# First matmul of four expert passes as half precision pairs, their matrices split during attention

## The reference, cut to what matters

```python
# attention: queries from layernorm(x), keys and values from layernorm(x) and from the context
sim  = einsum('bihd,bjhd->bhij', q1, concat([k1, k2])) * 64 ** -0.5
out  = einsum('bhij,bjhd->bihd', softmax(sim), concat([v1, v2]))
x    = x + tanh(g_xattn[0]) * (out.reshape(B, N1, h * d) @ Wo + bo)
# experts, on xf = layernorm(x): two of eight by the gate, and the shared one
for e in range(8):
    h   = gelu(xf @ w1[e] + b1[e])            # exact gelu
    out = out + combine[:, e:e + 1] * (h @ w2[e] + b2[e])
shared = gelu(xf @ ws1 + bs1) @ ws2 + bs2
x      = x + tanh(g_ffn[0]) * (out + shared)
```

## Time and profile before

| | |
|---|---|
| median of 3 runs | 157.3 us (156.89 to 157.64) |
| the profiled execution | 156.95 us, span of its trace 155.1 us |
| PE busy | 143.9 us (93%) |
| ACT busy | 115.1 us (74%) |
| POOL busy | 107.9 us (70%) |
| DVE busy | 103.5 us (67%) |
| granted TensorE clock | 1.00 over the span |

### The profile page before, as it was taken

One profiled execution on the slowest core, in us unless ns is written; L12 is line 12 of the kernel. 1 busy time (PEld: TensorE's weight loads), 2 busy tenths in 40 slices (PEclk: granted clock), 3 DMA queues, 4 the chain that ended last, 5 costly groups with the idle time before them and its releaser, 6 DMA issues.

```text
span 155.1 us, 4389 instructions
## 1 busy us (share of the span) xinstructions
PE 143.9 (93%) x1804; PEld 111.4 (72%) x1804; DVE 103.5 (67%) x215; ACT 115.1 (74%) x191; POOL 107.9 (70%) x95
## 2 busy tenths in 40 slices
PE   7789699979899999999898799999999999999992
PEld 5434354547566667657686698999999999989992
DVE  0779898888777686887763363834643779896631
ACT  3466789998988988887859988645567598968720
POOL 5506999777676667857798878965398089688730
PEclk9999999999999999999999999999999999999999
DMA  5679996000000000000000000030000000100001
GB/s 139 200 268 276 277 351 208 1 4 0 4 2 8 0 4 0 4 0 4 0 4 0 4 0 4 16 119 0 4 0 0 6 2 9 29 0 0 4 0 34
DMA packets 10253, 7.71 MB, mean 50 GB/s; under 512 B 1101, under 2 KB 8442, under 8 KB 10234
## 3 DMA queue, kind: packets, MB, share of 16 engines
q1 hardware_dynamic: 10234, 7.44, 15.8%
HBM read 7.18 MB, written 0.26 MB: 48 GB/s over the span
## 4 chain that ended last, share of the span: by engine, by line
PE 73%; DVE 10%; ACT 9%; issue 2%; DMA 2%; POOL 1%; SPq 0%; DVEq 0%; ACTq 0%
PE banks L1279 12%; PE banks L991 10%; PE banks L993 9%; PE banks L992 9%; PE banks L1242 5%; DVE part L821 4%; PE banks L1170 4%; ACT prob L646 3%; PE banks L1172 3%; PE banks L1171 3%; PE banks L1120 3%; PE banks L1190 2%; ACT v_hi L635 2%; DMA wf<-in_ctx_dram 2%; ACT p_hi L654 2%
## 5 line engine op out<-in xcount | busy, mean ns | idle before, releaser
L554 POOL TENSOR_TENSOR p_lo<-prob,p_hi 128x1024 f16<-128x1024 f32 x23 | 49.0, 2133 | 15.7 <-ACT p_hi L654 15.5
L710 ACT ACTIVATE prob<-banks,b1T 128x256 f32<-128x256 f32 x72 | 28.4, 475 | 12.8 <-PE banks L993 9.3
L646 ACT ACTIVATE prob<-banks 128x1024 f32<-128x1024 f32 x24 | 24.6, 1023 | 8.1 <-PE banks L1138 8.1
L821 DVE TENSOR_REDUCE part<-banks 128x2 f32<-128x1024 f32 (+1 forms) x24 | 29.0, 1216 | 1.1 <-PE banks L1093 1.0
L654 ACT ACTIVATE p_hi<-prob 128x1024 f16<-128x1024 f32 x24 | 25.4, 1057 | 0.8
L569 POOL TENSOR_TENSOR k_both<-prob,k_both 128x1024 f16<-128x1024 f32 x8 | 17.6, 2194 | 4.2 <-ACT k_both L718 3.2
L1279 PE MATMUL banks<-ring,prob 128*128 128x128 f32 x160 | 19.6, 276 | 0.0
L1170 PEld LDWEIGHTS banks<-v_hi,p_hi 128*128 128x128 f16 x192 | 17.4, 98 | 2.9 <-issue 2.5
L1170 PE MATMUL banks<-v_hi,p_hi 128*128 128x65 f16 x192 | 19.2, 195 | 0.0
L1171 PE MATMUL banks<-v_lo,p_hi 128*128 128x64 f16 x192 | 19.1, 193 | 0.0
L1172 PE MATMUL banks<-v_hi,p_lo 128*128 128x65 f16 x192 | 19.1, 194 | 0.0
(11 more groups left out here) (155 smaller groups left out, 343.8 us busy)
## 6 DMA issues: line engine op xcount, KB each, us to landing
ring<-in_L_ffn_w_dram SPq DMA_DIRECT2D x16, 256.0 KB, 5.3
wf<-in_ctx_dram SPq DMA_DIRECT2D x2, 256.0 KB, 5.3
ring<-in_L_xattn_Wk_dram SPq DMA_DIRECT2D x2, 256.0 KB, 4.7
ring<-in_L_xattn_Wv_dram SPq DMA_DIRECT2D x2, 256.0 KB, 7.1
ring<-in_L_ffn_ws_dram SPq DMA_DIRECT2D x2, 256.0 KB, 6.7
x_sb<-in_x_dram SPq DMA_DIRECT2D x1, 256.0 KB, 3.0
ring<-in_L_xattn_Wq_dram SPq DMA_DIRECT2D x1, 256.0 KB, 5.0
wo<-in_L_xattn_Wo_dram SPq DMA_DIRECT2D x1, 256.0 KB, 7.8
```

Source lines behind the costliest of these rows:

```text
L554: nc.gpsimd.tensor_tensor(p_lo[:, u % RINGP, :, :].rearrange("p a n -> p (a n)"), prob[:, u % RINGE, :], p_hi[:, u % RINGP, :, :].rearrang ...
L646: nc.scalar.activation(prob[:, u % RINGE, :], units(u).rearrange("p a n -> p (a n)"), ACT.Exp, scale=DH ** -0.5 / S_SCORE).then_inc(exp_do ...
L710: nc.scalar.activation(hid[:, k % NHID, c * T1:(c + 1) * T1], span(2 * (k % 2), HC * T1)[:, c * T1:(c + 1) * T1], ACT.Gelu, bias=b1T[:, e ...
L821: nc.vector.tensor_reduce(dst, src, AX_X, ALU.max).then_inc(part_done, 1)
```

## The change

All first matmuls become pairs. The first matrices of passes 1 to 4 are split during attention instead of in the FFN: hi by GpSimd in steps 7, 10, 13 and 16, after that step's `prob_lo`, and lo by VectorE at the end of steps 9, 12, 15 and 18. `split_after_use` and its semaphores go. The second matrix of pass 1, which was split there too, joins the list of ScalarE and VectorE, and that of pass 8, which only full precision passes use, leaves it, so that list still has seven.

```diff
-H32 = (1, 2, 3, 4)
-EARLY = 1 + len(H32)
-
-H32_SPLIT = [(1, 0), (2, 0), (1, 1), (3, 0), (4, 0)]
-H32_STEP = [FFN0 + 2, FFN0 + 3, FFN0 + 5, FFN0 + 6, FFN0 + 7]
+EARLY = 5
+EARLY_HI_STEP = (7, 10, 13, 16)
+EARLY_LO_STEP = (9, 12, 15, 18)
...
-W2_STEP = {2: FFN0 + 2, 3: FFN0 + 3, 4: FFN0 + 6, 5: FFN0 + 7, 6: FFN0 + 8, 7: FFN0 + 9, 8: FFN0 + 10}
+W2_STEP = {1: FFN0 + 2, 2: FFN0 + 3, 3: FFN0 + 6, 4: FFN0 + 7, 5: FFN0 + 8, 6: FFN0 + 9, 7: FFN0 + 10}
...
+        def early_part(j):
+
+            return 2 if j < 1 else 1
...
             def early_hi(j):
 
                 pool.wait_ge(ld_f[j], 32)
-                nc.gpsimd.tensor_tensor(flat(wf[:, 0, EORDER[j], :, :]), flat(ring_f(j)),
-                                        c_sw[:, :].broadcast_to([P, 2 * 512]), ALU.mult).then_inc(e_hi, 1)
+                n = early_part(j)
+                nc.gpsimd.tensor_tensor(flat(wf[:, 0, EORDER[j], 0:n, :]), flat(ring_f(j)[:, 0:n, :]),
+                                        c_sw[:, :].broadcast_to([P, n * 512]), ALU.mult).then_inc(e_hi, 1)
...
-            def split_after_use(m):
...
                 if i == 1:
                     early_lo(0)
-                if i in H32_STEP:
-                    split_after_use(H32_STEP.index(i))
+                if i in EARLY_HI_STEP:
+                    early_hi(EARLY_HI_STEP.index(i) + 1)
...
-                                             scale=1.0 if k in H32 else 1.0 / (S_ACTV * S_W)).then_inc(gelu_done, 1)
+                                             scale=1.0 / (S_ACTV * S_W)).then_inc(gelu_done, 1)
...
+                if i in EARLY_LO_STEP:
+                    j = EARLY_LO_STEP.index(i) + 1
+                    dve.wait_ge(e_hi, j + 1)
+                    expert_lo(j, slice(0, early_part(j))).then_inc(ed_lo, 1)
                 for j in W1_LATE:
...
-                    elif k in H32:
-                        pe.wait_ge(ld_f[k], 32)
+                    elif k < EARLY:
+                        pe.wait_ge(ed_lo, k)
                     elif k < NE:
                         pe.wait_ge(w1_lo, k - EARLY + 1)
-                    elif k - NE in H32:
-                        pe.wait_ge(h32_lo, H32_SPLIT.index((k - NE, 0)) + 1)
...
-                        dst = span(2 * (k % 2), HC * T1)[:, c * T1:(c + 1) * T1]
-                        if k in H32:
-                            last = nc.tensor.matmul(dst, ring_f(k)[:, 0, cols], x2T[:, tok], start=True, stop=True)
-                        else:
-                            last = three(dst, (wf[:, 0, e, 0, cols], wf[:, 1, e, 0, cols]),
-                                         (x2h[:, 0, tok], x2h[:, 1, tok]))
+                        last = three(span(2 * (k % 2), HC * T1)[:, c * T1:(c + 1) * T1],
+                                     (wf[:, 0, e, 0, cols], wf[:, 1, e, 0, cols]),
+                                     (x2h[:, 0, tok], x2h[:, 1, tok]))
```

More of the change, by code:

```diff
@@ L360, in block_kernel @@
         e_scaled, e_hi, e_lo = sem("e_scaled"), sem("e_hi"), sem("e_lo")
-        h32_hi, h32_scaled, h32_lo = sem("h32_hi"), sem("h32_scaled"), sem("h32_lo")
+        ed_lo = sem("ed_lo")
         hh_act = sem("hh_act")
@@ L1268, in _ @@
                             pe.wait_ge(w2_lo, W2_LATE.index(k % NE) + 1)
-                        elif (k % NE, 1) in H32_SPLIT:
-                            pe.wait_ge(h32_lo, H32_SPLIT.index((k % NE, 1)) + 1)
                         pe.wait_ge(hl_done, hid_splits(k))
```

## The result

The changed kernel takes 159.56 us (median of six executions, 158.62 to 160.22) against 156.86 before: a ratio of 1.0158, 95% interval 1.0109 to 1.0206. It is slower, as forecast, and inside the range; the size is +2.7 us where +1.5 was forecast. The profiled execution, at 158.62 us with a span of 156.8 (before: 156.95 and 155.1), shows only +1.7 of it. The rest is a second effect, which the listed executions show: three have a mean granted clock of 0.999 to 1.000 and take 158.6 to 159.1, with a median of 158.73 (+1.9), and three have 0.988 to 0.989 and take 160.0 to 160.2.

The account below looks back on a forecast made before the run. TensorE was taken to bound the kernel (73% of the chain's span). Attention's loss of 3.34 us less the FFN's gain of 1.84 made +1.5 us, forecast as 158.6 us, range 156.7 to 160.0.

Parts of the forecast that it names:

- The FFN's gain: FFN, passes 1 to 4: first matmuls as twelve half precision products instead of four full-precision ones, gaining 1.84 us.
- no Gelu is waited for: FFN: Gelus stay ahead of the products needing them; TensorE waiting for one would take from the gain, unpriced.
- GpSimd's multiplications: Attention, steps 7, 10, 13, 16: four of 1.04 us each fit GpSimd's idle time and cost nothing; without cover 4.2 us.
- The hold: Attention: each VectorE subtraction waits until GpSimd's running probability remainder ends, then needs 0.55 us; chance 0.69 as worked out.
- x: Attention: how late VectorE's next instruction, a value tile's remainder, begins after each held subtraction; taken as 1.89 us.
- The three losses: Attention: TensorE waits on late VectorE work following steps 9, 12 and 15, losing 0.36, 1.10 and 1.88 us, sum 3.34.
- step 18: Attention: the last subtraction makes a maximum 1.48 us late, but existing waits and idle time absorb it; cost nothing.
- the unheld subtraction: Rival, attention: subtractions run beside GpSimd's remainder, x = 0.61; end -1.2 us, 155.7 to 156.1; chance 0.13.
- GpSimd going first: Rival, attention: GpSimd's early multiplication gets in before the held subtraction, x = 3.01; +4.9 us, 161.8 to 162.2; chance 0.03.
- visible loads: Rival, FFN: weight loads of the pairs not hidden, a pass takes 2.62 us; +6.7 us, about 163.9; chance 0.01.
- the fall of the clock behind the 2 us stop: Attention, step 15: a granted clock below 1.00 after TensorE's stop would add to the loss; a sign of wrong, unpriced.

Follow-up runs that it names:

- the kernel with only that stop: The kernel with the subtractions in the gaps, but pass 3's subtraction put back to the end of step 15, its hi in step 14: 157.06 us, ratio 1.0028.
- the kernel with the subtractions in the gaps: Changed kernel with hi moved to steps 9, 12, 15, lo to 10, 13, 16, and pass 4 split in the FFN: 155.22 us, ratio 0.9888.
- the second measurement: The changed kernel run once more, unaltered: 158.57 us, ratio 1.0111 to the kernel before.

## Why the prediction was right, and where its size was short

The FFN's gain was forecast at 1.84 us and is 1.83 in the profile. With passes of 1.31 us the loads of their twelve weights do not show, and no Gelu is waited for. GpSimd's multiplications were forecast to cost nothing, and the kernel without the subtractions shows no cost. The hold was inferred from two FFN rows for a remainder that they did not show, and it came out: the subtractions end 0.54 to 0.56 us after the remainder, and the first makes VectorE late by x = 1.89 (51.62 against 49.55 plus the 0.18 of this execution). They begin 0.55 us into the remainder, not 0.7, and so their rows are 2.13 us long, not about 2.0; the end counts, and it did not move. The three losses were forecast at 0.36, 1.10 and 1.88 and are 0.35, 1.19 and 1.83, at the places named; step 18 costs nothing, as forecast. Together that is +1.54 in the profiled execution, where the forecast has 3.34 - 1.84 = +1.50; its other 0.18 us lie ahead of the first subtraction. The queue does not make up the loss of step 15 later: at full clock the kernel with only that stop takes as long as the one before beside it (156.9), while the kernel with the subtractions in the gaps takes 1.84 less than the one before (155.22 against 157.06).

Of the rivals, the unheld subtraction is excluded by the four rows of 2.13 us, GpSimd going first by the 1.49 us at 51.11, visible loads by the pass of 1.31 us.

What was short is the sum: it put every term at a granted clock of 1.00, and the fall of the clock behind the 2 us stop stood among what would make it wrong, without a price. A low clock costs 1.35 to 1.64 us (the difference of the two medians in each line of the table, before rounding), and it came in 9 of the 28 executions with the stop open. It came in three of the six that gave the result and moves their median up by 0.8, from 158.73 to 159.56. At full clock the changed kernel is 1.6 us above before in the second measurement and 1.9 in the first, against +1.5. That the result stayed inside the range is in part luck: with a fourth low execution the median would have been about 160.0, the range's end (an estimate from the low executions on record), and with one of six, as in the second measurement, it is 158.57. That the stop brings the clock down is shown by filling it; why it does so in some executions and not in others stays open.

## What to carry to other kernels

Before an instruction is put into an engine's free time, look at what the other engines do at that moment. Here a subtraction of 0.68 us with two SBUF inputs, issued on VectorE inside a GpSimd instruction of 2.13 us, held VectorE to the end of that instruction and 0.55 us beyond. The place of the same instructions decided between 1.8 us less than before (in the gaps) and 1.6 to 1.9 more (at full clock, 2.7 in the result). Follow the delay through the in-order queues to the first wait with no margin; that, not the instruction's length, is the price. And when a new stop of TensorE appears, price the clock behind it too, or fill the stop.

## What the runs showed that was not expected

In the one trace that shows it, the clock fell not during the stop but 1.3 us after TensorE had gone back to work, and stayed at half for the 3.4 us up to 76.0. With a stop of 2.08 us it fell in 9 of 28 executions, while in the kernel before, whose TensorE stops for 0.22 us there, none of the 41 executions that ran beside these experiments was below 0.997.
